# Attention pipeline: a step's scores placed ahead of its turned scores on TensorE, and the sum ahead of the exponential on ScalarE

## Chip, cores and metric

One core of a Trainium2 chip runs the whole program. The metric is the device time of one execution in microseconds (us); less is better. The times before are three executions of the kernel, and the time is their median.

## What is computed

The program is a small network over `x` of 2 x 1024 tokens with 128 features: a feed-forward part, a Mamba part, a second feed-forward part, a mixture of experts, attention, and the mixture of experts again. The change lies in the attention, which is, for each of 2 batches and 16 heads of width 64 (32 heads in all, `h` = 0 to 31):

```python
dots = einsum('bhid,bhjd->bhij', q, k) * SCALE          # 1024 x 1024 per head
diag = diagonal(softmax(dots))
keep = abs((diag - mean(diag)) / std(diag, ddof=1)) <= 1.5
valid = keep[..., :, None] & keep[..., None, :]
attn = softmax(where(valid, dots, -1e30))
attn = where(any(valid), attn, 0.0)
out = (attn @ v) @ w_out.T + b_out
```

## The kernel before

Everything stays in fp32; a product of two fp32 operands is made of three matmuls on halves rounded to fp32r (hi x hi, lo x hi, hi x lo). The engines are programmed by hand: each has its own instruction stream, executed in the order in which it is written, and semaphores tie the streams together.

**Steps.** A head is cut into 8 blocks of 128 rows or keys. All engines run over the same counter `t`, one step per block. A kind of work with offset `AT_X` handles in step `t` block `(t - AT_X) % 8` of head `(t - AT_X) // 8`. The ones that matter here:

- *Scores* (offset 0, written S(t) below): PE computes `dots` for 128 query rows into a PSUM tile of 1024 columns, in three pairs of matmuls on the two row halves of the array (L1969, L1970). DVE takes the block's diagonal out of it (`diagonal`, L2267, result `at_neg_diag`), ACT computes the exponential with that as its bias and sums each row (`sums`, L2169), which gives the diagonal of the first softmax.
- *Best* (offset 13, B(t)): one matmul pair (L2009, L2010), and DVE's masked row maximum (L2276, result `at_row_max`).
- *Turned scores* (offset 22, T(t)): PE computes the transposed block less the row maximum, four pairs (L2019, L2020 and L1890 with `at_shift_row`). ACT turns it into `at_e` (`exps`, L2179), DVE rounds that to `at_e_hi` (the cast, L2397), POOL forms the rest `at_e_lo` (L2422).
- *Weigh* (offset 24, two steps after the turned scores): PE multiplies `at_e_hi` and `at_e_lo` with the values into `at_pv_ps` (L1890), three pairs in a straight part ahead of B(t) and three in a turned part behind it.

So the streams meet in steps 22 to 255, in which a step has scores, turned scores, best and, from step 24, weigh. Before that only scores and best run, behind it only turned scores, weigh and the last of best.

**Per step, before.** PE: T(t), S(t), straight weigh, B(t), turned weigh. ACT: `exps`(t), then `sums`(t). DVE: `diagonal`(t), small statistics, the cast of `at_e`(t), best(t). Some steps have more: once per head PE projects q and k of a head (`qk`, in step 8h-3), and at the start of the next step ACT rounds it (L2154) and DVE takes the rest (L2251), ahead of that step's diagonal; in two steps of every 32 the same happens with the values of four heads (L1939; ACT L2161, DVE L2257); once in 16 steps there is an output projection, which DVE adds to `x` (L2371). Once per head ACT copies `at_pv_ps` out (L2218).

**PSUM slots.** Three tiles `at_ps0` to `at_ps2` serve all of these in turn. `attention_slots` writes down the order in which they are taken, and PE waits (`slot_free`) before a use of slot n for the reader of slot n-3: for scores the end of `sums`, for turned scores the end of `exps`, for best the end of DVE's best.

The waits that the argument needs:

```python
    # attention_act
    def sums(h, blk):
        act.wait_ge(sem["at_diag"], h * BLK + blk + 1)
    def exps(h, blk):
        act.wait_ge(sem["at_turned_scores"], e + 1)
        if e >= 2:
            act.wait_ge(sem["at_lo"], e - 2 + 1)
    # attention_dve
    def diagonal(h, blk):
        dve.wait_ge(sem["at_scores"], e + 1)
        ...
        if at := due(t, AT_TURNED, BLK):
            e = at[0] * BLK + at[1]
            dve.wait_ge(sem["at_exp"], e + 1)
```

Of the kernel before, what the change touches and what calls it, by code (L numbers as in the profile page):

```python
# [44 lines left out]
BLK = SEQ // P  # L45
# [1526 lines left out]
AT_SPLIT, AT_QK, AT_SCORES, AT_STATS, AT_MEAN, AT_SQUARE, AT_MASK, AT_BEST, AT_SHIFT = -6, -3, 0, 8, 9, 10, 11, 13, 21  # L1572
# [6 lines left out]
def due(t, offset, n=1):  # L1579

    h, k = divmod(t - offset, BLK)
    return (h, k) if 0 <= h < NH and k < n else None
# [27 lines left out]
def small_due(t):  # L1610

    for kind, offset in (("mean", AT_MEAN), ("square", AT_SQUARE), ("turn_mask", AT_MASK), ("turn_shift", AT_SHIFT)):
        if at := due(t, offset):
            return kind, at[0]
    return None


def attention_slots():

    order, number = [], {}  # L1620
    for t in range(AT_FIRST, AT_LAST):
        small, best = small_due(t), due(t, AT_BEST, BLK)
        if at := due(t, AT_TURNED, BLK):
            order.append([("turned_scores", *at)])
        if at := due(t, AT_SCORES, BLK):
            order.append([("scores", *at)])
        if small or best:
            order.append([(*small, 0)] if small else [])
            if best:
                order[-1].append(("best", *best))  # L1630
        if (h := qk_due(t)) is not None:
            order.append([("qk", h, 0)])
        if at := group_due(t):
            order.append([("values", *at)])
        if (h := pair_due(t)) is not None:
            order.append([("out", h, 0)])
    for n, keys in enumerate(order):
        for key in keys:
            number[key] = n
    return order, number  # L1640
# [230 lines left out]
def attention_pe(c, m):  # L1871
# [227 lines left out]
    for t in range(AT_FIRST, AT_LAST):  # L2099
        weighed, tested = due(t, AT_PV, BLK), due(t, AT_BEST, BLK)  # L2100
        apart = bool(weighed and tested)
        if at := due(t, AT_TURNED, BLK):
            turned_scores(*at)
        if at := due(t, AT_SCORES, BLK):
            scores(*at)
        if at := due(t, AT_MEAN):
            mean(at[0])
        if at := due(t, AT_SQUARE):
            square(at[0])
        if at := due(t, AT_MASK):  # L2110
            turn_mask(at[0])
        if at := due(t, AT_SHIFT):
            turn_shift(at[0])
        if apart:
            weigh(*weighed, False)
        if tested:
            best(*tested)
        for turned in (False, True):
            if (h := qk_due(t)) is not None:
                if apart:  # L2120
                    project(h, turned)
                elif not turned:
                    project_alone(h)
                    if h == 1:
                        fill_wait(pe, c, m.ps[2][:, HALF[0]], 27)
            if at := group_due(t):
                if apart:
                    values(*at, turned)
                elif not turned:
                    values_alone(*at)  # L2130
            if (h := pair_due(t)) is not None:
                if apart:
                    project_out(h, turned)
                elif not turned:
                    project_out_alone(h)
            if apart and not turned:
                weigh(*weighed, True)
        if weighed and not apart:
            weigh_alone(*weighed)
            if weighed == (LAST, BLK - 1):  # L2140
                fill_wait(pe, c, m.ps[(m.slot_no["out", LAST, 0] + 1) % 3][:, HALF[0]], 15)


def attention_act(c, m):
    act, sem = c.act, c.sem

    def slot(kind, h, k=0):
        return m.ps[m.slot_no[kind, h, k] % 3]

    def round_qk(h):  # L2150
        act.wait_ge(sem["at_qk"], h + 1)
        if h >= SLOTS:
            act.wait_ge(sem["at_turned_scores"], (h - SLOTS) * BLK + BLK)
        act.eng.activation(m.qk[h % SLOTS][:, HI, :], slot("qk", h)[:], ACT.Copy).then_inc(sem["at_qk_hi"])  # L2154

    def round_values(g, part):
        blks = slice(part * (BLK // 2), (part + 1) * (BLK // 2))
        act.wait_ge(sem["at_v"], 2 * g + part + 1)
        if g:
            act.wait_ge(sem["at_pv"], (g * GROUP - 1) * BLK + blks.stop)  # L2160
        act.eng.activation(m.v_hi[:, blks, :, 0, :].rearrange("p b h d -> p (b h) d"),  # L2161
                           slot("values", g, part)[:].rearrange("p (h d) -> p h d", d=HD),
                           ACT.Copy).then_inc(sem["at_v_hi"])

    def sums(h, blk):
        s = h % SLOTS
        ps = slot("scores", h, blk)
        act.wait_ge(sem["at_diag"], h * BLK + blk + 1)
        act.eng.activation(ps[:], ps[:], ACT.Exp, scale=SCALE, bias=m.small["neg_diag"][s][:, blk:blk + 1],  # L2169
                           accum_out=m.small["sums"][s][:, blk:blk + 1]).then_inc(sem["at_sum"])  # L2170

    def exps(h, blk):
        e = h * BLK + blk
        act.wait_ge(sem["at_turned_scores"], e + 1)
        act.wait_ge(sem["at_xn_lo"], NCH)
        act.wait_ge(sem["at_wv_lo"], 1)
        if e >= 2:
            act.wait_ge(sem["at_lo"], e - 2 + 1)
        act.eng.activation(m.e[e % 2][:], slot("turned_scores", h, blk)[:], ACT.Exp, scale=SCALE,  # L2179
                           bias=m.small["dropped"][h % SLOTS][:, blk:blk + 1]).then_inc(sem["at_exp"])  # L2180

    def last_inverses():

        act.wait_ge(sem["at_ones"], 2)
        for hf in range(2):
            act.eng.activation(m.last_inv[HD:, HALF[hf]], m.pv_ps[HD:, HALF[hf]], ACT.Ln,
                               bias=m.tiny[HD:, 0:1]).then_inc(sem["at_pv_out"])
            act.wait_ge(sem["at_pv_out"], LAST + 2 * hf + 1)
            act.eng.activation(m.last_inv[HD:, HALF[hf]], m.last_inv[HD:, HALF[hf]], ACT.Exp,
                               scale=-1.0).then_inc(sem["at_pv_out"])  # L2190

    def parts_of(whole, parts, done):
        act.eng.activation(parts[:, 0:1], whole[:], ACT.Copy).then_inc(sem["at_dev"])
        act.wait_ge(sem["at_dev"], done + 1)
        act.eng.activation(parts[:, 1:2], parts[:, 0:1].bitcast(F32), ACT.Identity, scale=-1.0,
                           bias=whole[:, 0:1]).then_inc(sem["at_dev"])

    def row_parts(h):
        i = h % SLOTS
        act.wait_ge(sem["at_stats"], STATS * h + 2)  # L2200
        parts_of(m.ones_col["row_sum"][i], m.halves["row_sum"][i], DEVS * h)

    def deviations(h):
        i = h % SLOTS
        act.wait_ge(sem["at_stats"], STATS * h + 3)
        act.eng.activation(m.small["dev2"][i][:], m.small["diag"][i][:], ACT.Square, bias=m.ones_col["neg_mean"][i][:, 0:1],
                           accum_out=m.ones_col["sq_sum"][i][:, 0:1]).then_inc(sem["at_dev"])
        act.wait_ge(sem["at_dev"], DEVS * h + 3)
        parts_of(m.ones_col["sq_sum"][i], m.halves["sq_sum"][i], DEVS * h + 3)

    for t in range(AT_FIRST, AT_LAST):
        if at := due(t, AT_PV_OUT):
            h = at[0]
            act.wait_ge(sem["at_pv"], h * BLK + BLK)
            if h:
                act.wait_ge(sem["at_norm"], h)
            if h < LAST:
                act.eng.activation(m.pv_sb[:], m.pv_ps[:], ACT.Copy).then_inc(sem["at_pv_out"])  # L2218
            else:
                last_inverses()  # L2220
        if (h := qk_due(t - 1)) is not None:
            round_qk(h)
            if h == 1:
                attention_later_norm_act(c, m)
        if at := group_due(t - 1):
            round_values(*at)
        if at := due(t, AT_TURNED, BLK):
            exps(*at)
        if at := due(t, AT_SCORES, BLK):
            sums(*at)  # L2230
        if at := due(t, AT_STATS):
            row_parts(at[0])
        if at := due(t, AT_MEAN):
            deviations(at[0])
    act.wait_ge(sem["x_attn"], ATTN_SUMS)
# [436 lines left out]
```

## Time and profile before

| | |
|---|---|
| three executions | 1890.33, 1894.06, 1895.96 us |
| median | 1894.06 us |
| the profiled execution: its time | 1891.39 us |
| its span, first to last instruction | 1889.9 us |
| mean granted TensorE clock | 0.990 of full |
| busy share of the span: PE, DVE, ACT, POOL | 94%, 70%, 61%, 62% |
| steps 22 to 255 of the attention | 777.0 to 1678.9 us, 234 steps |

The share of an engine is its busy time over the whole span, a mean over stages with different limits. The time of the profiled execution is 2.67 us under the median.

### The profile page before, as it was taken

The page shows a single profiled execution, that of the slowest core. Times are in us where ns is not written, and L with a number is a line of the kernel's source. Part 1 is how long each engine was busy: PE and PEld are TensorE (multiplying, and loading weights), DVE is VectorE, ACT ScalarE, POOL GpSimd, SP SyncE. Part 2 cuts the span into 40 slices and gives each one's busy share as a digit, 9 for nine tenths or more (in the row PEclk, how much of TensorE's full clock was granted, in tenths as well). Part 3 has the DMA queues.
Part 4 walks back from the last instruction along what each step waited for, and adds up shares of the span by engine and source line. Part 5 has one row for each costly group of instructions (what it writes and reads, how often), then busy time and mean ns, then how long its engine had stood idle before and what let it go on. Part 6 is the DMA issues. An engine that isn't in the chain of part 4 may idle for free. (4 is left out here: it accounts for less than half of the span.)

```text
span 1889.9 us, 29839 instructions
## 1 busy us (share of the span) xinstructions
PE 1781.0 (94%) x11031; PEld 1211.9 (64%) x11031; DVE 1330.9 (70%) x2493; ACT 1150.2 (61%) x1715; POOL 1172.7 (62%) x660
## 2 busy tenths in 40 slices
PE   9998999888999897899999999999999999999888
PEld 5883444334786674577777777777777777765466
DVE  5627899996445764777777777777777777778676
ACT  5326777853435447676767676766766676653554
POOL 5551677874554452377776776777767777677354
PEclk9999999999999999999999999999999999999999
DMA  3000000000001003121222222121212121200100
GB/s 100 1 1 1 1 0 1 1 0 1 1 1 50 1 1 100 39 60 48 60 53 55 54 54 65 44 70 42 66 36 71 48 60 47 58 24 12 50 6 17
DMA packets 43664, 66.03 MB, mean 35 GB/s; under 512 B 24768, under 2 KB 26176, under 8 KB 43264
## 3 DMA queue, kind: packets, MB, share of 16 engines
q1 hardware_dynamic: 43056, 63.54, 12.9%
q8 instruction: 88, 1.44, 0.3%
q10 hardware_dynamic: 432, 0.59, 0.1%
q14 instruction: 56, 0.46, 0.1%
q0 software_dynamic: 32, 0.00, 0.0%
HBM read 29.05 MB, written 1.24 MB: 16 GB/s over the span
## 5 line engine op out<-in xcount | busy, mean ns | idle before, releaser
L2422 POOL TENSOR_TENSOR at_e_lo<-at_e,at_e_hi 128x1024 fp32r<-128x1024 f32 x256 | 613.0, 2395 | 300.8 <-DVE at_e_hi L2397 296.4
L2179 ACT ACTIVATE at_e<-at_ps,at_dropped 128x1024 f32<-128x1024 f32 x256 | 285.6, 1116 | 222.0 <-PE at_ps L1890 201.4
L2276 DVE CUSTOM_DVE_ANT_0 at_ps<-at_ps,at_mask 128x1024 f32<-128x1024 f32 x256 | 313.3, 1224 | 4.1 <-PE at_ps L2010 4.1
L2169 ACT ACTIVATE at_ps<-at_ps,at_neg_diag 128x1024 f32<-128x1024 f32 x256 | 278.6, 1088 | 36.7 <-DVE at_neg_diag L2267 36.4
L2397 DVE CAST at_e_hi<-at_e 128x1024 fp32r<-128x1024 f32 x256 | 233.8, 913 | 23.1 <-ACT at_e L2179 19.5
L1969 PE MATMUL at_ps<-at_kq,at_qk 64*128 64x512 f32 x768 | 221.0, 395 | 8.6 <-DMA at_kq<-at_qk 3.0
L2019 PE MATMUL at_ps<-at_qk,at_kq 64*128 64x512 f32 x768 | 224.7, 399 | 1.6 <-DVE at_row_max L2276 1.2
L1890 PE MATMUL at_pv_ps<-at_e_hi,at_v_hi 64*128 64x512 f32 x980 | 225.7, 453 | 0.2 <-issue 0.2
L2020 PE MATMUL at_ps<-at_kq,at_qk 64*128 64x512 f32 x768 | 224.8, 399 | 0.0
L1970 PE MATMUL at_ps<-at_qk,at_kq 64*128 64x512 f32 x768 | 221.1, 395 | 0.0
L1056 POOL TENSOR_TENSOR mb_work<-mb_work,mb_c 128x1024 f32<-128x1024 f32 x64 | 151.8, 2373 | 97.7 <-DVE mb_work L1025 97.6
L421 POOL TENSOR_TENSOR ffn_lo<-ffn_hid,ffn_hi 128x512 fp32r<-128x512 f32 x96 | 127.2, 1328 | 132.1 <-DVE ffn_hi L338 132.1
L1890 PE MATMUL at_pv_ps<-at_e_hi,at_v_lo 64*64 64x512 f32 x980 | 195.4, 391 | 0.0
L1890 PE MATMUL at_pv_ps<-at_e_lo,at_v_hi 64*128 64x512 f32 x980 | 194.5, 389 | 0.0
L2267 DVE CUSTOM_DVE_ANT_0 at_junk_diag<-at_ps,ident 128x128 bf16<-128x128 f32 x256 | 74.0, 289 | 146.8 <-PE at_ps L1970 144.4
L1969 PEld LDWEIGHTS at_ps<-at_kq,at_qk 64*128 64x128 f32 x768 | 139.4, 185 | 47.9 <-DMA at_kq<-at_qk 12.8
L2019 PEld LDWEIGHTS at_ps<-at_qk,at_kq 64*128 64x128 f32 x768 | 139.7, 185 | 39.6 <-issue 7.9
L1500 POOL TENSOR_TENSOR moe_hid_lo<-moe_prod,moe_hid_hi 128x512 fp32r<-128x512 f32 (+1 forms) x72 | 92.8, 1290 | 95.5 <-ACT moe_hid_hi L1332 95.5
L1025 DVE TENSOR_TENSOR_SCAN mb_work<-mb_work,mb_u_ps 128x1024 f32<-128x1024 f32 x64 | 146.3, 2286 | 6.4 <-PE mb_y_ps L652 1.2
L338 DVE CAST ffn_hi<-ffn_hid 128x512 fp32r<-128x512 f32 x96 | 64.0, 670 | 120.9 <-ACT ffn_hid L309 119.6
L2020 PEld LDWEIGHTS at_ps<-at_kq,at_qk 64*128 64x128 f32 x768 | 139.7, 185 | 2.3 <-issue 1.0
L1970 PEld LDWEIGHTS at_ps<-at_qk,at_kq 64*128 64x128 f32 x768 | 139.4, 185 | 0.9
(392 smaller groups left out, 4158.7 us busy)
## 6 DMA issues: line engine op xcount, KB each, us to landing
at_kq<-at_qk SPq DMA_DIRECT2D x128, 256.0 KB, 4.0
at_mask<-at_mask_dram SPq DMA_DIRECT2D x32, 256.0 KB, 3.6
at_recips<-at_recip_row SPq DMA_DIRECT2D x31, 256.0 KB, 4.4
ffn_h_raw<-in_h SPq DMA_DIRECT2D x2, 1024.0 KB, 7.6
at_head_w_raw<-in_w_qkv SPq DMA_DIRECT2D x32, 64.0 KB, 3.9
x<-in_x SPq DMA_DIRECT2D x4, 256.0 KB, 4.7
moe_gate_in<-in_gate_in SPq DMA_DIRECT2D x2, 512.0 KB, 3.9
moe_up_in<-in_up_in SPq DMA_DIRECT2D x2, 512.0 KB, 4.4
```

Source lines behind the costliest of these rows:

```text
L1025: dve.eng.tensor_tensor_scan(m.state[i % MB_STATES_HELD], m.d_a[i % MB_DECAYS], m.u_ps[:], 0.0, ALU.mult, ALU.add).then_inc(sem["mb_scan"])
L1056: pool.eng.tensor_tensor(m.state[i % MB_STATES_HELD], m.state[i % MB_STATES_HELD], m.c_sb[i % 3], ALU.mult).then_inc(sem["mb_hc"])
L1890: mm = pe.eng.matmul(bank, w[rows], moving[rows], start=first, stop=last)
L1969: pe.eng.matmul(ps[:, HALF[0]], own[TOP, q, rows], swapped[TOP, k, HALF[0]], start=(n == 0), stop=(n == 2))
L1970: mm = pe.eng.matmul(ps[:, HALF[1]], swapped[LOW, q, rows], own[LOW, k, HALF[1]], start=(n == 0), stop=(n == 2))
L2019: pe.eng.matmul(ps[:, HALF[0]], swapped[TOP, k, keys], own[TOP, q, HALF[0]], start=(n == 0), stop=False)
L2020: pe.eng.matmul(ps[:, HALF[1]], own[LOW, k, keys], swapped[LOW, q, HALF[1]], start=(n == 0), stop=False)
L2169: act.eng.activation(ps[:], ps[:], ACT.Exp, scale=SCALE, bias=m.small["neg_diag"][s][:, blk:blk + 1], accum_out=m.small["sums"][s][:, blk: ...
L2179: act.eng.activation(m.e[e % 2][:], slot("turned_scores", h, blk)[:], ACT.Exp, scale=SCALE, bias=m.small["dropped"][h % SLOTS][:, blk:blk ...
L2276: dve.eng.tensor_tensor_reduce(out=ps[:], in0=ps[:], in1=m.mask[h % 2][:], scale=1.0, scalar=-BIG, op0=ALU.add, op1=ALU.max, accum_out=m.s ...
L2397: dve.eng.tensor_copy(m.e_hi[e % 3][:], m.e[e % 2][:]).then_inc(sem["at_hi"])
L2422: pool.eng.tensor_tensor(m.e_lo[e % 3][:], m.e[e % 2][:], m.e_hi[e % 3][:].bitcast(F32), ALU.subtract).then_inc(sem["at_lo"])
```

## The change

Three loops are written in another order; no instruction is added, removed or resized.

```diff
 # attention_slots
     for t in range(AT_FIRST, AT_LAST):
         small, best = small_due(t), due(t, AT_BEST, BLK)
+        if at := due(t, AT_SCORES, BLK):
+            order.append([("scores", *at)])
         if at := due(t, AT_TURNED, BLK):
             order.append([("turned_scores", *at)])
-        if at := due(t, AT_SCORES, BLK):
-            order.append([("scores", *at)])
 # attention_pe
+        if at := due(t, AT_SCORES, BLK):
+            scores(*at)
         if at := due(t, AT_TURNED, BLK):
             turned_scores(*at)
-        if at := due(t, AT_SCORES, BLK):
-            scores(*at)
 # attention_act
+        if at := due(t, AT_SCORES, BLK):
+            sums(*at)
         if at := due(t, AT_TURNED, BLK):
             exps(*at)
-        if at := due(t, AT_SCORES, BLK):
-            sums(*at)
```

PE at the start of a plain step in the attention, before (L2019, L2020 and L1890 are the turned scores, L1969 and L1970 the scores):

```order
3078 L2019 MATMUL at_ps<-at_qk,at_kq 128x512 [waits at_exp]
3079 L2020 MATMUL at_ps<-at_kq,at_qk 128x512
3080 L2019 MATMUL at_ps<-at_qk,at_kq 128x512
3081 L2020 MATMUL at_ps<-at_kq,at_qk 128x512
3082 L2019 MATMUL at_ps<-at_qk,at_kq 128x512
3083 L2020 MATMUL at_ps<-at_kq,at_qk 128x512
3084 L1890 MATMUL at_ps<-at_shift_row,at_minus 128x512 x2
3085 L1969 MATMUL at_ps<-at_kq,at_qk 128x512 [waits at_sum]
3086 L1970 MATMUL at_ps<-at_qk,at_kq 128x512
```

The same place in the changed kernel:

```order
3078 L1969 MATMUL at_ps<-at_kq,at_qk 128x512 [waits at_sum]
3079 L1970 MATMUL at_ps<-at_qk,at_kq 128x512
3080 L1969 MATMUL at_ps<-at_kq,at_qk 128x512
3081 L1970 MATMUL at_ps<-at_qk,at_kq 128x512
3082 L1969 MATMUL at_ps<-at_kq,at_qk 128x512
3083 L1970 MATMUL at_ps<-at_qk,at_kq 128x512
3084 L2019 MATMUL at_ps<-at_qk,at_kq 128x512 [waits at_exp]
3085 L2020 MATMUL at_ps<-at_kq,at_qk 128x512
```

The two groups have changed places, and each keeps its wait for its own PSUM reader.

ACT in the step of the statistics and the next, before (L2179 is `exps`, L2169 `sums`):

```order
528 L2179 ACTIVATE at_e<-at_ps,at_dropped 128x1024 [waits at_lo,at_turned_scores]
529 L2169 ACTIVATE at_ps,at_sums<-at_ps,at_neg_diag 128x1024 [waits at_diag]
530 L2179 ACTIVATE at_e<-at_ps,at_dropped 128x1024 [waits at_lo,at_turned_scores]
531 L2169 ACTIVATE at_ps,at_sums<-at_ps,at_neg_diag 128x1024 [waits at_diag]
532 L2179 ACTIVATE at_e<-at_ps,at_dropped 128x1024 [waits at_lo,at_turned_scores]
```

And in the changed kernel:

```order
528 L2169 ACTIVATE at_ps,at_sums<-at_ps,at_neg_diag 128x1024 [waits at_diag]
529 L2179 ACTIVATE at_e<-at_ps,at_dropped 128x1024 [waits at_lo,at_turned_scores]
530 L2169 ACTIVATE at_ps,at_sums<-at_ps,at_neg_diag 128x1024 [waits at_diag]
531 L2179 ACTIVATE at_e<-at_ps,at_dropped 128x1024 [waits at_lo,at_turned_scores]
532 L2169 ACTIVATE at_ps,at_sums<-at_ps,at_neg_diag 128x1024 [waits at_diag]
```

Within a step the sum now stands ahead of the exponential.

DVE's stream is the same in both kernels. The tail of one step and the head of the next (L2267 diagonal, L2397 cast, L2276 best, L2257 rest of the values):

```order
1006 L2397 CAST at_e_hi<-at_e 128x1024 [waits at_pv,at_exp]
1007 L2276 ISA at_ps,at_row_max<-at_ps,at_mask 128x1024 [waits at_best]
1008 L2276 ISA at_row_max 128x1
1009 L2257 TENSOR_TENSOR at_v_lo<-at_ps,at_v_hi 128x1024 [waits at_v_hi]
1010 L2267 ISA at_junk_diag,at_neg_diag<-at_ps,ident 128x128 [waits at_diag,at_scores]
1011 L2267 ISA at_neg_diag 128x1
1012 L2397 CAST at_e_hi<-at_e 128x1024 [waits at_pv,at_exp]
```

Nothing moved here: the diagonal of a step stands ahead of the step's cast, and the next diagonal behind best. POOL's and the DMA queue's streams are the same in both kernels as well.

## Rows read from the trace of the kernel before

**Rows 1.** The page: the span, and busy time, share and instructions of PE.
```profile
span 1889.9 us, 29839 instructions
PE 1781.0 (94%) x11031; PEld 1211.9 (64%) x11031; DVE 1330.9 (70%) x2493; ACT 1150.2 (61%) x1715; POOL 1172.7 (62%) x660
```

**Rows 2.** Busy time by stretch; columns as the first row says.
```profile
core 0: us, PE busy (x) PEld busy (x) DVE busy (x) ACT busy (x) POOL busy (x), PEclk, DMA share, GB/s
777.00:1678.90 901.90, 888.91 (x7558) 654.21 (x7560) 655.48 (x1575) 627.45 (x950) 645.61 (x318) 1.00 0.22 54
```

**Rows 3.** DVE in 776:1679: counts, ns min/median/max; idle before cast, before diagonal.
```profile
L2397 DVE CAST at_e_hi<-at_e x234: 650/695/2080, 777.2 to 1676.0; 128x1024 fp32r<-128x1024 f32 x117
...
  ACT at_e L2179: 8.4, 51
...
L2267 DVE CUSTOM_DVE_ANT_0 at_junk_diag<-at_ps,ident x234: 278/291/293, 777.0 to 1675.8; 128x128 bf16<-128x128 f32 x117
...
  PE at_ps L1970: 135.6, 160
```

**Rows 4.** Timeline, one plain step: start, duration (us), engine, line, idle before and releaser.
```profile
1353.41 1.12 ACT L2179 ACTIVATE at_e<-at_ps,at_dropped 128x1024 f32<-128x1024 f32 x1 [1.58 <-PE at_ps L1890]
...
1354.42 1.09 ACT L2169 ACTIVATE at_ps<-at_ps,at_neg_diag 128x1024 f32<-128x1024 f32 x1
...
1354.56 0.69 DVE L2397 CAST at_e_hi<-at_e 128x1024 fp32r<-128x1024 f32 x1 [0.17 <-ACT at_e L2179]
1355.17 1.23 DVE L2276 CUSTOM_DVE_ANT_0 at_ps<-at_ps,at_mask 128x1024 f32<-128x1024 f32 x1
1355.33 2.39 POOL L2422 TENSOR_TENSOR at_e_lo<-at_e,at_e_hi 128x1024 fp32r<-128x1024 f32 x1 [0.83 <-DVE at_e_hi L2397]
```

**Rows 5.** Timeline: a diagonal, the sum that waited for it, and ACT's next instruction.
```profile
1340.15 0.29 DVE L2267 CUSTOM_DVE_ANT_0 at_junk_diag<-at_ps,ident 128x128 bf16<-128x128 f32 x1 [1.86 <-PE at_ps L1970]
...
1340.48 1.09 ACT L2169 ACTIVATE at_ps<-at_ps,at_neg_diag 128x1024 f32<-128x1024 f32 x1 [1.03 <-DVE at_neg_diag L2267]
...
1341.50 0.19 ACT L2169 ACTIVATION_READ_ACCUMULATOR at_ps<-at_ps,at_neg_diag 128x1 f32 x1
1341.59 0.19 ACT L2193 ACTIVATE at_row_sum_parts<-at_row_sum 128x1 fp32r<-128x1 f32 x1
```

**Rows 6.** Timeline of DVE in the lead-in: best, and a diagonal that was ready behind it.
```profile
757.22 1.23 DVE L2276 CUSTOM_DVE_ANT_0 at_ps<-at_ps,at_mask 128x1024 f32<-128x1024 f32 x1 [1.83 <-PE at_ps L2010]
758.37 0.14 DVE L2276 DVE_READ_ACCUMULATOR2_ANT at_row_max<- 128x1 f32 x1
758.37 0.28 DVE L2267 CUSTOM_DVE_ANT_0 at_junk_diag<-at_ps,ident 128x128 bf16<-128x128 f32 x1
```

**Rows 7.** Timeline around a projection of q and k: PE, ACT's rounding, DVE's rest, diagonal.
```profile
1328.22 0.41 PE L1890 MATMUL at_ps<-at_xn_hi,at_head_w_hi 64*128 64x512 f32 x2
...
1328.45 0.40 PE L1890 MATMUL at_ps<-at_xn_hi,at_head_w_lo 64*128 64x512 f32 x2
...
1330.51 1.03 ACT L2154 ACTIVATE at_qk<-at_ps 128x1024 fp32r<-128x1024 f32 x1 [1.64 <-PE at_ps L1890]
...
1331.58 1.22 DVE L2251 TENSOR_TENSOR at_qk<-at_ps,at_qk 128x1024 fp32r<-128x1024 f32 x1 [1.86 <-ACT at_qk L2154]
...
1332.72 0.28 DVE L2267 CUSTOM_DVE_ANT_0 at_junk_diag<-at_ps,ident 128x128 bf16<-128x128 f32 x1
```

**Rows 8.** Timeline around the second half of the values: turned weigh, then ACT.
```profile
903.97 0.39 PE L1890 MATMUL at_pv_ps<-at_e_hi,at_v_hi 64*128 64x512 f32 x2
...
904.86 1.03 ACT L2218 ACTIVATE at_pv_sb<-at_pv_ps 128x1024 f32<-128x1024 f32 x1 [0.56 <-PE at_pv_ps L1890]
...
905.78 1.02 ACT L2161 ACTIVATE at_v_hi<-at_ps 128x1024 fp32r<-128x1024 f32 x1
```

**Rows 9.** Timeline: a cast that met POOL's work.
```profile
1299.48 2.40 POOL L2434 TENSOR_TENSOR at_heads_out<-at_pv_sb,at_recips 64x1024 f32<-64x1024 f32 x1
...
1301.28 1.15 DVE L2397 CAST at_e_hi<-at_e 128x1024 fp32r<-128x1024 f32 x1
```

**Rows 10.** Busy time by stretch in the lead-in, columns as in rows 2.
```profile
748.00:752.00 4.00, 2.34 (x14) 1.11 (x14) 1.70 (x11) 3.08 (x8) 0.00 (x0) 0.90 0.96 234
752.00:754.50 2.50, 2.50 (x14) 1.60 (x14) 0.84 (x5) 1.67 (x3) 0.00 (x0) 0.50 0.38 73
757.00:776.00 19.00, 13.03 (x84) 7.48 (x84) 14.29 (x45) 11.91 (x24) 0.00 (x0) 1.00 0.05 15
```

**Rows 11.** Timeline of PE in 752 to 754: two successive matmuls of one array half.
```profile
752.61 0.62 PE L1969 MATMUL at_ps<-at_kq,at_qk 64*128 64x512 f32 x1
...
753.03 0.62 PE L1969 MATMUL at_ps<-at_kq,at_qk 64*128 64x512 f32 x1
```

## The prediction

> **What bounds the kernel now.** I read the page first, then the stretch of the attention by busy time, then the order of the four streams, and last the timeline of single steps. The page has PE busy for 94% of the span [rows 1]. In the stretch where all kinds of attention work run together, steps 22 to 255, PE is busy 888.9 of 901.9 us, while DVE is busy 655.5, ACT 627.5 and POOL 645.6 [rows 2]. So PE sets the pace there, and a step costs 901.9 / 234 = 3.85 us on average (234 by the counts of [rows 3]). The reader should see two things in that. First, at most 901.9 - 888.9 = 13.0 us can be won here by feeding PE better. Second, the three other engines have slack, but slack of an engine is not slack of a chain that runs through several engines: what matters is how long the longest ring of waits is that has to be gone round once per step.
>
> **The rings, before.** DVE does in a step: diagonal(t), cast(t), best(t). ACT does exp(t), sum(t). The cast needs exp(t), the sum needs diagonal(t). In the plain step of [rows 4] the exponential starts at 1353.41, the cast at 1354.56, best at 1355.17, and the sum follows the exponential without holding any of them up. The diagonal of the next step waits behind best, but the exponential of that step does not wait for that diagonal; it waits for PE ("1.58 <-PE"). A ring through diagonal, sum, exp, cast, best and the next diagonal exists, but it spans two steps: the sum of step t stands ahead of the exponential of step t+1. DVE has time to spare in it: it sat idle 135.6 us before the diagonal, in 160 cases, for PE [rows 3].
>
> **The change on ACT.** Here is the whole of the matter. With the sum ahead of the exponential of its own step, and DVE's order as it was, the ring closes within one step: diagonal(t) on DVE, sum(t) on ACT, exp(t) on ACT, cast(t) on DVE, best(t) on DVE, diagonal(t+1). Each element is queued behind the one before it or waits for it, and no buffer can loosen that, because DVE reaches diagonal(t+1) only behind best(t). Its length, start to start:
>
> - diagonal to the sum waiting for it: 1340.15 to 1340.48, 0.33 us [rows 5].
> - sum to ACT's next instruction, past the accumulator read: 1340.48 to 1341.59, 1.11 us [rows 5].
> - exponential to the cast that waits for it: 1353.41 to 1354.56, 1.15 us [rows 4].
> - cast to best: 0.61 us [rows 4].
> - best to a diagonal that is ready: 757.22 to 758.37, 1.15 us [rows 6].
>
> The sum is 4.35 us per step. That is more than the average step of 3.85 with all its additions, and much more than a plain one. So the ring becomes the bound, and PE waits.
>
> **What PE does meanwhile.** I checked that PE doesn't lengthen the ring. Counting from diagonal(t): successive pairs start 0.23 us apart [rows 7]. B(t) starts at about 0.15, when the previous best is out; the turned weigh follows to 1.2; S(t+1) needs sum(t), whose accumulator read ends at 1.54, and runs 1.6 to 2.3; T(t+1) needs exp(t), started at 1.44 and 1.12 long, and runs 2.6 to 3.5; the straight weigh to 4.2; then B(t+1) waits for best(t). S(t+1) is wanted at 4.35 and T(t+1) at 5.79. Both have two microseconds in hand. So the earlier scores, the PE half of the change, cost nothing and give nothing: their diagonal has to wait for DVE anyway. The small statistics stand between diagonal and cast, where DVE now idles about two microseconds, and cost nothing. The transfers of q, k and shift rows have longer steps to land in, so their waits go.
>
> **What still adds to the ring.** DVE work that stands ahead of a diagonal isn't covered.
>
> - q and k: the projection takes its slot three behind, which is now the scores' (it was the turned scores'), so it starts at sum(t)'s end, 1.6. From its first matmul to ACT's rounding are 2.29 us, to DVE's rest 1.07 more, to the diagonal 1.14 more [rows 7]: 1.6 + 4.50 = 6.10 instead of 4.35, so 1.75 us. 28 of these in the stretch (h = 4 to 31): 49.0 us.
> - values, first half: the same shape, 1.75, 8 times: 14.0 us.
> - values, second half: ACT has the copy of `at_pv_ps` ahead of the rounding. Turned weigh at 2.3, copy 0.89 later, rounding 0.92 later [rows 8], then 1.07 and 1.14 as above: 6.32, so 1.97, 8 times: 15.8 us.
> - output projection: PE's part is done by the time best ends, DVE's addition of about 1.15 us (the 1.14 of rows of the same size) stays, 13 times: 15.0 us.
>
> **The sum.** 234 x 4.35 + 49.0 + 14.0 + 15.8 + 15.0 = 1017.9 + 93.8 = 1111.7 us for the stretch, against 901.9: 209.8 us longer. The steps ahead of it and behind it have no turned scores or no scores, so their streams are the same, and nothing is counted there. The profiled execution would go from 1891.4 to 2101 us; the median lies 2.7 above that execution, so the forecast is 1894.1 + 209.8 = 2104 us. The error to be expected: a step 0.1 shorter gives 2081; all additions at their bare DVE time of 1.14 give 57 x 1.14 = 65.0, so 29 us less, 2075; at twice their size, 94 more, 2198, which I find far because each link of them was read.
>
> **Two prices that rows bound from both sides.** The cast is 0.65 to 2.08 us long, median 0.70 [rows 3]. It is long when it meets POOL: at 1301.28 it took 1.15, with POOL's `at_heads_out` still running to 1301.88 [rows 9]. In the ring, POOL's `at_e_lo` starts 0.77 behind the cast's start and lasts 2.39 [rows 4], so it ends 3.16 behind it, 1.19 ahead of the next cast. I take the free value, 0.61 to best; the other end is 0.46 more in each step, 108 us. The Trainium skill, in "SBUF — State Buffer", section "Who interferes with whom", says that of two such instructions the later is blocked for all of the earlier; the rows agree with it, and by it the sum stays as it is unless POOL runs late by that 1.19 us.
>
> The second is TensorE's clock. In the stretch it was 1.00 throughout at 98.6% busy [rows 2]. Afterwards PE would be busy 889 of 1112 us, 80%, with three short pauses a step. The nearest rows speak for a clock that stays: 757 to 776 had 13.0 of 19.0 us busy at 1.00, but 752 to 754.5 had 0.50 (1.2 GHz), right behind a stretch busy only 2.34 of 4.0 us [rows 10]. I take 1.00. The Trainium skill, in "TensorE: Matmul & The Clock Gate", section "A second HAM failure mode: psum-queue depth-cycling", says that a kernel which pauses between groups while it cycles PSUM banks swings between the two levels. That speaks against this kernel; the rival below prices it.
>
> **The rivals.**
>
> - *The ring does not close, and PE gets its scores' readers earlier.* This would be so if the round trip were shorter than 3.85 us, for instance if DVE's diagonal could pass a waiting cast. Then what remains of the change is that the diagonal comes four pairs, 0.9 us, earlier, and some of the 135.6 us of DVE's waiting and PE's 13.0 us go: 1881 to 1894 us. Against it: even without any of the semaphore time, by durations alone, the ring is 0.29 + 1.09 + 1.12 + 0.69 + 1.23 = 4.42, and less the overlaps of neighbours on one engine about 4.0, over 3.85. 3%.
> - *The casts meet POOL* in every step: 2104 + 108 = 2212 us. For it: the 2.08 maximum; against it: the 1.19 us of room. 6%; in part of the steps it lies between.
> - *The clock falls to 1.2 GHz in the attention.* Then pairs start 0.42 us apart [rows 11], 14 pairs a step are 5.9 us, PE is the bound again, and if that held throughout the stretch would be 234 x 1.5 = 360 us longer still, 2465; in a third of the steps, 2225. Against it: the 19 us at 69% busy and full clock. 5%.
> - *The additions hide* in the ring more than I see, or the links are each some hundredths shorter: 2060 to 2080. 6%.
>
> **How the numbers follow.** The forecast's own case has 80%: 2104 us, with about 2080 to 2150 around it. The range is drawn to 2078 and 2165, so that it takes in links a tenth shorter and casts that meet POOL in half of the steps, and leaves out most of the rivals. A difference of 0.3%, 5.7 us, is about what a measurement of this kernel can tell. Faster by more than that 0.02 and within it 0.01, both from the first rival; slower 0.97.
>
> **What would show it.** In the profile of the changed kernel: ACT's sum waits for the diagonal in nearly all of 234 steps; the cast waits for the exponential about 2 us each (it was 8.4 us in all the stretch, in 51 cases [rows 3]); DVE's idle before the diagonal for PE is almost gone; PE is busy about 80% of the stretch and waits for `at_sum`, `at_exp` and `at_row_max`; diagonals are 4.35 us apart in plain steps, and about 1.7 more behind a projection. The stretch is about 1112 us, and the stages outside it unchanged within a microsecond or two. The prediction is wrong if the diagonals are 3.3 us apart in plain steps (no ring), if casts last over 1 us, or if the clock shows less than 1.00 there.

## The result and the profile after

| | before | changed |
|---|---|---|
| median | 1892.68 us (4 executions) | 2103.32 us (4 executions, 2102.09 to 2104.64) |
| ratio, with its 95% interval | | 1.1117 [1.1104, 1.1131] |
| span of the profiled execution | 1889.9 us | 2100.8 us |
| steps 22 to 255 | 902 us | 1114 us |
| mean granted TensorE clock | 0.990 | 0.991 |

The forecast was 2104 us in a range of 2078 to 2165, a growth of 209.8 us; measured are 210.6. Of all executions that the runs below rest on two were slow, one of the kernel before (2846.07 us) and one of it with a small instruction more (2438.51 us, granted clock 0.65), and no ratio rests on them.

First the page of the changed kernel, which answers to [rows 1]:

```profile
span 2100.8 us, 29839 instructions
PE 1875.1 (89%) x11031; PEld 1205.4 (57%) x11031; DVE 1289.2 (61%) x2493; ACT 1145.5 (55%) x1715; POOL 1170.3 (56%) x660
```

The stretch of the joint steps, which answers to [rows 2], with the same columns (us, then busy time and count of PE, PEld, DVE, ACT, POOL, then the granted clock):

```profile
774.80:1888.60 1113.80, 983.74 (x7562) 647.61 (x7562) 614.31 (x1575) 624.11 (x950) 642.65 (x318) 1.00 0.18 44
```

It is 211.9 us longer than before (1113.8 against 901.9), and the span is 210.9 longer, so everything outside the stretch is unchanged within about a microsecond. No engine got more instructions. One plain step in the timeline of the changed kernel, DVE and ACT, to be laid beside [rows 4 to 6]:

```profile
1505.65 0.28 DVE L2267 CUSTOM_DVE_ANT_0 at_junk_diag<-at_ps,ident 128x128 bf16<-128x128 f32 x1
...
1505.97 1.09 ACT L2169 ACTIVATE at_ps<-at_ps,at_neg_diag 128x1024 f32<-128x1024 f32 x1 [1.20 <-DVE at_neg_diag L2267]
...
1507.08 1.11 ACT L2179 ACTIVATE at_e<-at_ps,at_dropped 128x1024 f32<-128x1024 f32 x1
...
1508.22 0.69 DVE L2397 CAST at_e_hi<-at_e 128x1024 fp32r<-128x1024 f32 x1 [1.97 <-ACT at_e L2179]
1508.83 1.23 DVE L2276 CUSTOM_DVE_ANT_0 at_ps<-at_ps,at_mask 128x1024 f32<-128x1024 f32 x1
...
1509.97 0.29 DVE L2267 CUSTOM_DVE_ANT_0 at_junk_diag<-at_ps,ident 128x128 bf16<-128x128 f32 x1
```

These starts are 0.32, 1.11, 1.14, 0.61 and 1.14 us apart, 4.32 together. Who waits for whom in the stretch shows the same ring (engine, waiting, waited for: us in total, times, longest):

```profile
DVE at_e_hi L2397 <- ACT at_e L2179: 432.8, 233, 2.3
ACT at_ps L2169 <- DVE at_neg_diag L2267: 428.2, 234, 3.4
...
PEld at_ps L1969 <- ACT at_ps L2169: 43.0, 66, 0.7
ACT at_qk L2154 <- PE at_ps L1890: 42.6, 28, 1.5
PEld at_ps L2019 <- ACT at_e L2179: 42.2, 101, 0.5
```

The cast now waits for ACT in 233 of 234 steps (51 before, [rows 3]), ACT's sum waits for DVE in all 234, and DVE no longer waits for PE before a diagonal at all. DVE and ACT each wait some 430 us for the other. That is what a closed ring looks like: two engines at 55% of their time, each idle because of the other.

### The profile page after: what moved, and what is told of

It reads as the page before. It is cut to its first block and busy times, and to the rows that moved or that the text cites. A ratio compares the mean times of both kernels' runs of the same rounds, so it can differ in the third digit from the quotient of the medians.

```text
span 2100.8 us, 29839 instructions
## 1 busy us (share of the span) xinstructions
PE 1875.1 (89%) x11031; PEld 1205.4 (57%) x11031; DVE 1289.2 (61%) x2493; ACT 1145.5 (55%) x1715; POOL 1170.3 (56%) x660
## 3 DMA queue, kind: packets, MB, share of 16 engines
HBM read 29.05 MB, written 1.24 MB: 14 GB/s over the span
## 5 line engine op out<-in xcount | busy, mean ns | idle before, releaser
L2169 ACT ACTIVATE at_ps<-at_ps,at_neg_diag 128x1024 f32<-128x1024 f32 x256 | 278.6, 1088 | 437.2 <-DVE at_neg_diag L2267 436.9
L2397 DVE CAST at_e_hi<-at_e 128x1024 fp32r<-128x1024 f32 x256 | 201.8, 788 | 446.4 <-ACT at_e L2179 443.9
L2276 DVE CUSTOM_DVE_ANT_0 at_ps<-at_ps,at_mask 128x1024 f32<-128x1024 f32 x256 | 313.7, 1226 | 4.3 <-PE at_ps L2010 4.2
L2179 ACT ACTIVATE at_e<-at_ps,at_dropped 128x1024 f32<-128x1024 f32 x256 | 283.6, 1108 | 41.9 <-PE at_ps L1890 25.4
L1969 PE MATMUL at_ps<-at_kq,at_qk 64*128 64x512 f32 x768 | 235.8, 414 | 26.7 <-ACT at_ps L2169 19.9
L2019 PE MATMUL at_ps<-at_qk,at_kq 64*128 64x512 f32 x768 | 234.4, 411 | 5.1 <-DVE at_row_max L2276 1.8
L1970 PE MATMUL at_ps<-at_qk,at_kq 64*128 64x512 f32 x768 | 236.3, 415 | 0.0
L2020 PE MATMUL at_ps<-at_kq,at_qk 64*128 64x512 f32 x768 | 233.8, 410 | 0.0
L1890 PE MATMUL at_pv_ps<-at_e_hi,at_v_hi 64*128 64x512 f32 x980 | 223.5, 443 | 0.8 <-DVE at_e_hi L2397 0.8
L1890 PE MATMUL at_pv_ps<-at_e_lo,at_v_hi 64*128 64x512 f32 x980 | 199.0, 390 | 0.0
L1890 PE MATMUL at_pv_ps<-at_e_hi,at_v_lo 64*64 64x512 f32 x980 | 198.9, 390 | 0.0
L1969 PEld LDWEIGHTS at_ps<-at_kq,at_qk 64*128 64x128 f32 x768 | 134.3, 186 | 91.4 <-ACT at_ps L2169 47.8
L2019 PEld LDWEIGHTS at_ps<-at_qk,at_kq 64*128 64x128 f32 x768 | 130.0, 185 | 78.1 <-ACT at_e L2179 43.3
L652 PE MATMUL mb_y_ps<-mb_work,ident 128*128 128x512 f32 x256 | 131.8, 601 | 8.3 <-DVE mb_dtx L949 6.8
L1970 PEld LDWEIGHTS at_ps<-at_qk,at_kq 64*128 64x128 f32 x768 | 134.3, 187 | 2.7
L2020 PEld LDWEIGHTS at_ps<-at_kq,at_qk 64*128 64x128 f32 x768 | 130.0, 185 | 2.7
```

The lines of the kernel that those rows point to most:

```text
L1890: mm = pe.eng.matmul(bank, w[rows], moving[rows], start=first, stop=last)
L1969: pe.eng.matmul(ps[:, HALF[0]], own[TOP, q, rows], swapped[TOP, k, HALF[0]], start=(n == 0), stop=(n == 2))
L1970: mm = pe.eng.matmul(ps[:, HALF[1]], swapped[LOW, q, rows], own[LOW, k, HALF[1]], start=(n == 0), stop=(n == 2))
L2019: pe.eng.matmul(ps[:, HALF[0]], swapped[TOP, k, keys], own[TOP, q, HALF[0]], start=(n == 0), stop=False)
L2020: pe.eng.matmul(ps[:, HALF[1]], own[LOW, k, keys], swapped[LOW, q, HALF[1]], start=(n == 0), stop=False)
L2276: dve.eng.tensor_tensor_reduce(out=ps[:], in0=ps[:], in1=m.mask[h % 2][:], scale=1.0, scalar=-BIG, op0=ALU.add, op1=ALU.max, accum_out=m.s ...
```

## The experiments

All distances between diagonals below are read from DVE's diagonals (L2267) in the timeline of each kernel, steps 22 to 255, as means over the steps with the same `t mod 8` (us). Step 3 has the output projection every second time, 5 the projection of q and k; 6 and 7 are those without values, and without step 254, which has more to do (5.56 in the changed kernel).

| t mod 8 | 0 | 1 | 2 | 4 | 5 | 6 | 7 |
|---|---|---|---|---|---|---|---|
| before | 3.22 | 3.42 | 3.42 | 3.31 | 5.34 | 2.99 | 3.71 |
| changed | 4.32 | 4.33 | 4.33 | 4.32 | 6.20 | 4.32 | 4.33 |
| PE half alone | 3.77 | 4.19 | 4.20 | 3.99 | 7.73 | 2.66 | 4.28 |
| ACT half alone | 4.53 | 4.53 | 4.53 | 4.53 | 7.18 | 4.52 | 4.53 |
| changed, best ahead of the cast | 3.48 | 3.41 | 4.76 | 3.26 | 6.17 | 3.18 | 3.42 |

**The two halves apart.** The first kernel has only the order of PE and of the slots:

```diff
-        if at := due(t, AT_TURNED, BLK):
-            turned_scores(*at)
         if at := due(t, AT_SCORES, BLK):
             scores(*at)
+        if at := due(t, AT_TURNED, BLK):
+            turned_scores(*at)
```

> Only the PE half: scores ahead of turned scores in the slots and on PE; ACT keeps the exponential ahead of the sum. Theory R, as predicted (the slowdown is the ring diagonal, sum, exp, cast, best, closed on ACT alone; the PE half costs nothing): no ring in one step, so 1881 to 1894 us. Rival P (PE's order closes a ring of its own over the PSUM slot): T(t)'s last pair starts 1.5 us behind S(t)'s first, exp starts 0.43 later, the sum 1.01 behind it and ends 1.28 later, and only then S(t+1) may write the slot: 4.2 to 4.3 us per plain step, relaxed in the steps after an extra slot, so 2040 to 2110 us, with PE waiting for at_sum (L2169) before L1969.

Measured: 2096.98 us, 1.1095 [1.1075, 1.1114] of before. The rival is right, and by its numbers: a plain step is 4.19 us. From its timeline:

```profile
1505.19 1.11 ACT L2179 ACTIVATE at_e<-at_ps,at_dropped 128x1024 f32<-128x1024 f32 x1 [1.16 <-PE at_ps L1890]
...
1506.20 1.08 ACT L2169 ACTIVATE at_ps<-at_ps,at_neg_diag 128x1024 f32<-128x1024 f32 x1
...
1507.19 0.20 ACT L2169 ACTIVATION_READ_ACCUMULATOR at_ps<-at_ps,at_neg_diag 128x1 f32 x1
...
1507.45 0.50 PE L1969 MATMUL at_ps<-at_kq,at_qk 64*128 64x512 f32 x1 [0.59 <-ACT at_ps L2169]
```

The exponential waits for the turned scores, the sum (whose diagonal has long been there) stands behind it, and the next step's scores wait for the sum to give back the PSUM tile; the turned scores stand behind those scores. The starts of exponential, sum and scores are 1.01 and 1.25 us apart, and the next exponential starts 1.93 us after the scores, at 1509.38: 4.19 together. It is a second ring, through PE, ACT and a slot, without DVE. The steps with a projection of q and k grew most, from 5.34 to 7.73, which is 70 of the 206 us.

The second has only ACT's order:

```diff
-        if at := due(t, AT_TURNED, BLK):
-            exps(*at)
         if at := due(t, AT_SCORES, BLK):
             sums(*at)
+        if at := due(t, AT_TURNED, BLK):
+            exps(*at)
```

> Only the ACT half: the sum ahead of the exponential; slots and PE as before. Theory R: the ring is there whatever PE does, 4.32 us a plain step, 2100 us. A finer reading of R: here T(t+1), which waits for exp(t), stands ahead of S(t+1) on PE, so the diagonal comes exp(t)'s end plus seven pairs (1.5 us) plus 0.43 us later: about 4.5 us a step, and the projections start at the exponential's end instead of the sum's, 1 us later 44 times: 2150 to 2195 us, with DVE idle before the diagonal for PE (L1970). If the ACT half were harmless: 1893 us.

Measured: 2210.47 us, 1.1691 [1.1671, 1.1710], above the finer reading's end by 15 us. The step is 4.53, as it said. From its timeline:

```profile
1501.26 1.11 ACT L2179 ACTIVATE at_e<-at_ps,at_dropped 128x1024 f32<-128x1024 f32 x1
...
1502.42 0.49 PE L2019 MATMUL at_ps<-at_qk,at_kq 64*128 64x512 f32 x1 [0.40 <-ACT at_e L2179]
...
1503.91 0.39 PE L1969 MATMUL at_ps<-at_kq,at_qk 64*128 64x512 f32 x1
...
1504.35 0.29 DVE L2267 CUSTOM_DVE_ANT_0 at_junk_diag<-at_ps,ident 128x128 bf16<-128x128 f32 x1
```

The turned scores start when the exponential has left their tile, the scores follow, and the diagonal comes 0.44 us after the last pair, 0.2 later than best (read accumulator 1504.15) would have allowed it. One point was off: DVE's wait was expected to be listed under PE; it is too short in most steps and stands there with 15 us only, over the whole execution. The excess over the range is where the expectation added nothing: a step with an output projection takes 7.03 us, 2.50 more than a plain one, against 1.22 more in the changed kernel, which over 13 of them is 17 us. Each half alone costs 206 and 320 us; together they cost 211. So the halves are not additive: with the sum first, the early scores are worth 107 us.

**The ring opened on DVE.** The changed kernel, with two blocks of DVE's loop exchanged, and the kernel before with the same exchange:

```diff
+        if at := due(t, AT_BEST, BLK):
+            best(*at)
         if at := due(t, AT_TURNED, BLK):
             ...
             dve.eng.tensor_copy(m.e_hi[e % 3][:], m.e[e % 2][:]).then_inc(sem["at_hi"])
-        if at := due(t, AT_BEST, BLK):
-            best(*at)
```

> The changed kernel, and on DVE best(t) ahead of the cast of its step, all else equal. The same instructions on every engine. Theory R: best (1.15 us) leaves the ring and runs while DVE waits for the exponential; the ring is 0.33 + 1.11 + 1.15 + about 0.6 = 3.2 us, under PE's own 3.3 in a plain step, so PE is the bound again: 1880 to 1915 us. If the loss came from the order on PE, from the clock or from contention, it stays near 2100.

> The kernel before, with only DVE's best(t) ahead of the cast. Shows what that order is worth by itself: PE is the bound there with 13 us of idle in the stretch, so 1885 to 1905 us; a gain in e3 over this one would be the scores' order, a loss its cost.

Measured: 1974.01 us, 1.0437 [1.0420, 1.0455], and 1905.08 us, 1.0075 [1.0058, 1.0091]. One instruction moved out of the ring takes 129 us off the changed kernel, and plain steps fall from 4.32 to between 3.18 and 3.5, as expected. But the time is 59 us above the end of the forecast's range, for two reasons that the distances show: step 2 lasts 4.76 (39 us more than before over the stretch), and steps 5 and those with values keep the lengths of the changed kernel (6.17, and 6.13 and 6.41 with values, against 5.34, 4.94 and 5.12 before; the means with values include steps 22 and 23), since their projections still wait in PE's slot order for the sum (steps 5 to 7 are 42 us more than before). Moving best is no gain in itself: it costs the kernel before 14 us (1890.76 without the exchange), with 4.12 for 3.42 in step 2 and 4.19 for 4.55 in step 3. Against that kernel the changed order still costs 69 us, 3.6%.

**A small instruction more.** The same DVE instruction in three places; it reads the identity and writes a column that nothing reads:

```diff
         if at := due(t, AT_BEST, BLK):
             best(*at)
+        if due(t, AT_SCORES, BLK) and due(t, AT_TURNED, BLK):
+            dve.eng.tensor_reduce(m.pad[t % 8][:], c.ident[:], AX.X, ALU.add)
```

> The changed kernel with one small extra instruction on DVE (a row sum over 128 columns of the identity into an unused column, about 0.2 us by the spacing of the diagonal) behind best in each of the 234 joint steps, ahead of the next diagonal. Theory R: it is on the ring, and every step grows by its length: 234 x 0.2 = 47 us, 2140 to 2160 us. If DVE were not on the path (PE or PSUM slots set the pace): no change, 2103.

> The same extra instruction in the changed kernel, but right behind the diagonal, ahead of the cast, where DVE waits over 2 us for the exponential. Theory R: hidden, 2103 us within 6. If DVE's total work counted: as p1.

(there the two new lines stand behind `diagonal(*at)`)

> The kernel before with the extra instruction behind best, as in p1. Theory R: there the ring spans two steps and PE is the bound; DVE sat idle 136 us before its diagonals in 160 steps, so most of it is absorbed: 1892 to 1905 us.

> Only the PE half (as the first experiment), with the small DVE instruction behind best in each joint step. If that kernel's bound is the ring turned scores, exp, sum, slot, scores, which has no DVE in it: within 8 us of 2097. If it were DVE's ring through best, as in the full change: 33 us more, 2130.

| kernel | without | with |
|---|---|---|
| changed, behind best | 2103.3 | 2136.85, 1.1288 [1.1269, 1.1307] of before |
| changed, behind the diagonal | 2103.3 | 2102.02, 1.1103 [1.1084, 1.1121] |
| before, behind best | 1892.1 | 1893.69, 1.0000 [0.9989, 1.0011] |
| PE half alone, behind best | 2097.0 | 2098.30, 1.1088 [1.1071, 1.1105] |

Where it stands in the timeline of the first:

```profile
1502.24 0.28 DVE L2401 TENSOR_REDUCE at_pad<-ident 128x1 f32<-128x128 f32 x1
1502.44 0.28 DVE L2267 CUSTOM_DVE_ANT_0 at_junk_diag<-at_ps,ident 128x128 bf16<-128x128 f32 x1
```

It takes 0.20 us of DVE's time, and the plain step grows from 4.32 to 4.52. The total grew by 33.5 and not by 47, 3 us below the expected range, because in step 5 and in those with values DVE waits behind it anyway (6.20 with and without). The other three places cost nothing that can be told from zero. These four are the sharpest evidence of the study: the same instruction is paid in full ahead of the diagonal and free right behind it, 0.3 us later; and it is free behind best where only PE's order was changed, so that kernel, as slow as the full change, is slow by a ring that this place on DVE is not in.

**What held step 2.** In the third kernel's trace the `keeps` instruction L2306 (128x8) stands out:

```profile
L2306 DVE TENSOR_SCALAR at_keep<-at_dev,at_limit,at_varies x32: 291/1382/2074, 751.6 to 1766.1; 128x8 f32<-128x8 f32 x32
```

(ns: shortest, median, longest; before it is 290, 299, 920.) Two kernels put it elsewhere in DVE's step. Behind the cast:

```diff
             negate_square(at[0])
-            keeps(at[0])
 ...
             dve.eng.tensor_copy(m.e_hi[e % 3][:], m.e[e % 2][:]).then_inc(sem["at_hi"])
+        if at := due(t, AT_SQUARE):
+            keeps(at[0])
```

> The changed kernel with best ahead of the cast, and the four small instructions of keeps (once per head) behind the cast. In the version without that, its third one took 1.38 us instead of 0.3 beside POOL's at_e_lo, and steps of t mod 8 = 2 lasted 4.76 us instead of 3.4. If POOL's work over the shared port is the cause and the cast starts POOL anew behind it: 1.0 to 1.3 us less in 29 heads, 1936 to 1945 us. If those instructions only waited for something on PE or ACT: 1974.

and, together with the two reciprocal instructions, between best and the cast:

```diff
         if at := due(t, AT_BEST, BLK):
             best(*at)
+        if at := due(t, AT_SQUARE):
+            keeps(at[0])
+        if (at := due(t, AT_RECIP)) and at[0] < LAST:
+            ...
```

> The changed kernel with DVE's order diagonal, best, then keeps and the two small reciprocal instructions, then the cast (third experiment, with the statistics moved behind best but ahead of the cast). POOL's at_e_lo of the step before is then nearly over when keeps starts, 3.0 us behind the previous cast's start against its end at 3.16. If the shared port is what held keeps (1.38 us in the third experiment, 2.21 in the one with it behind the cast): keeps takes 0.3 to 0.5 us, steps of t mod 8 = 2 last 4.1 to 4.5 instead of 4.76, the clock stays at 1.00, and the time is 1955 to 1970 us. If something on PE or ACT held it, keeps stays long and the time at 1974 or above.

The first came out the other way from its forecast: 2089.78 us, 1.1050 [1.1033, 1.1067], 116 us slower than the kernel it was to mend. The second: 1964.34 us, 1.0379 [1.0362, 1.0397], 10 us faster, in its range. From the timeline of the first of them:

```profile
1504.10 0.69 DVE L2398 CAST at_e_hi<-at_e 128x1024 fp32r<-128x1024 f32 x1
1504.86 2.34 POOL L2423 TENSOR_TENSOR at_e_lo<-at_e,at_e_hi 128x1024 fp32r<-128x1024 f32 x1 [1.31 <-DVE at_e_hi L2398]
1505.02 2.21 DVE L2306 TENSOR_SCALAR at_keep<-at_dev,at_limit,at_varies 128x8 f32<-128x8 f32 x1
1507.26 0.17 DVE L2309 TENSOR_SCALAR at_dropped<-at_keep 128x8 f32<-128x8 f32 x1
...
1507.49 0.26 PE L1984 MATMUL at_ps<-ident,at_dropped 64*8 64x64 f32 x2 [3.25 <-DVE at_dropped L2309]
1507.59 0.79 PE L1890 MATMUL at_pv_ps<-at_e_hi,at_v_hi 64*128 64x512 f32 x2
```

An instruction on eight columns takes 2.21 us, and ends when POOL's does (1507.23 and 1507.20). In the third kernel it was the same: there `keeps` started at 1499.31, took 1.38 us and ended at 1500.69, and POOL's `at_e_lo` at 1500.66. The expectation had said that the cast "starts POOL anew behind it", and drew the wrong conclusion: right behind the cast is the one place where `keeps` is sure to meet all of `at_e_lo`. With it between best and cast, the median is 291 ns again, and step 2 is 4.42 us. That `keeps` is blocked for what is left of POOL's instruction is what the Trainium skill says in "SBUF — State Buffer", section "Who interferes with whom"; here 2.21, 1.38 and 0.29 us in three places agree with it. In the kernel with `keeps` behind the cast PE waits 3.25 us for the result (28 of 29 times; once 2.39), and its clock falls behind most of these waits.

The table's distances, taken for this kernel too, split its 116 us. Step 2 went from 4.76 to 7.12, 68 us over the stretch. Steps 3 and 4 grew by 36 and 7 us. In the 5 of 29 heads where the clock stayed at 1.00 behind the wait, step 2 is as long or nearly as long (7.15; 6.28 in the first), but steps 3 and 4 are as in the third kernel (3.19 to 3.22 and 3.32 or 3.33); in the other heads without an output projection step 3 takes 4.15 to 4.89. So about 68 us are the wait and about 43 the lower clock.

**Is the opposite direction better?** Since the change moved the scores earlier and lost, the last two moved them later in the kernel before, behind the straight weigh:

```diff
-        if at := due(t, AT_SCORES, BLK):
+        late = apart and t % BLK in (4, 6, 7) and due(t, AT_SCORES, BLK)
+        if (at := due(t, AT_SCORES, BLK)) and not late:
             scores(*at)
 ...
         if apart:
             weigh(*weighed, False)
+        if late:
+            scores(*late)
```

> The kernel before, with the scores moved the other way: behind the straight weigh, ahead of best, in the steps of t mod 8 = 4, 6, 7, which have no small product. Then four pairs instead of one lie between straight and turned weigh, and the pause before the turned weigh (0.1 us between pairs) goes in those; the sum and diagonal start 0.7 us later, for which the order exp, sum has room (diagonal to sum's end 1.6 us, needed 3.3 later). Gain about 60 x 0.1 = 6 us, with the pauses for the transfer of q and k untouched: 1883 to 1889 us beside 1892. If the later diagonal lengthens a ring: over 1892.

> The same also in the steps of t mod 8 = 0, where the first scores of a head wait for the transfer of q and k (0.86 us in the row read). The straight weigh would cover that wait, but it waits itself for ACT's copy of at_pv_ps there. Gain over the former 0 to 15 us: 1870 to 1887 us.

Measured: 1891.08 us, 1.0000 [0.9991, 1.0009], no change; and 1913.44 us, 1.0118 [1.0102, 1.0133], slower. In the first, PE's waits for its own straight weigh did shrink as meant, from 34.7 us in 146 cases to

```profile
PEld at_pv_ps L1890 <- PE at_pv_ps L1890: 21.5, 95, 0.3
...
PEld at_ps L1969 <- DMA at_kq<-at_qk: 14.1, 21, 1.4
...
PEld at_ps L1969 <- ACT at_ps L2172: 6.4, 29, 0.2
```

but 6.4 us of waits for the sum of a delayed step are new, and the wait for the transfer of q and k grew from 11.7 to 14.1 us in the weight loads and by 1.7 in the matmuls. The gain was given back within the head. In the second the straight weigh waits for ACT's copy of `at_pv_ps`, as feared: in one such step the copy ends at 1350.85 and the weigh starts at 1350.95, after 0.76 us without a matmul. The profile names no releaser for these waits (16 us in 21 cases); the kernel's order and this distance do. No version that ran beats the kernel before.

## Why the prediction was right, and where not

- *The ring.* Right in kind and size: 4.35 us predicted, 4.32 measured; 234 x 0.03 = 7 us too much.
- *The additions.* Projection of q and k: 1.75 predicted, 6.27 - 4.32 = 1.95 in a typical case. Its first matmul starts 1.68 us behind the diagonal, not 1.6, and the path to ACT is 2.39, not 2.29. Values: 1.75 and 1.97 predicted, 1.90 and 2.10 measured. Output: 1.15 predicted, 1.22 measured (5.54 in 11 of its 13 steps, 5.60 in two). Over 57 cases these are about 9 us too little. The two errors cancel nearly, and the stretch came out at 1113.8 for 1111.7. The good agreement of the total is partly luck.
- *PE's share.* Predicted 80% of the stretch, measured 983.7 of 1113.8, 88%. The step that failed is "PE would be busy 889": the busy time isn't a constant of the work. The first matmul after a pause is listed with 0.49 us instead of 0.39, and matmuls that overlapped each other's ends before now stand apart.
- *"So the earlier scores, the PE half of the change, cost nothing and give nothing."* This is the sentence that the runs refute. Alone, they cost 206 us by a ring that the prediction never looked for, and beside the sum's new place they give 107. What is true is less: in the changed kernel S(t+1) and T(t+1) are ready before the ring needs them. The total was right since, with the sum first, PE's ring is not closed: S(t+1) waits for a sum that stands ahead of the exponential. The third kernel shows it, as it has the same order on PE and ACT and plain steps of 3.18 to 3.5 us, where PE's ring alone had made them 4.19.
- *The rival of a gain* needed a diagonal that passes a waiting cast, or a shorter round trip. Neither is in the trace: the cast waited for the exponential in 233 of 234 steps, with the next diagonal behind it, and the round trip was 4.32. But the third kernel shows that closing wasn't the only danger: with that ring opened, the order still loses 4.4%.
- *Contention.* Casts stayed at 0.69 us (median 694 ns, one of 1923), so that rival had no part. *The clock* stayed at 1.00 in the stretch.

## What to carry to other kernels

When two instructions of one step change places on an in-order engine, ask for every instruction queued behind them on any engine which step's result it needs. A ring that spanned two steps may span one, and its length is then the price of each step, however idle the engines are. Write down the rings of an order, PSUM slots included, with their start-to-start distances; the trace of the kernel before has each of them, and the sum forecast a plain step here to 0.03 us. Halves of such a change must be judged apart and together, as they can compensate each other.

An instruction of 0.2 us put in at a suspected place tells cheaply whether that place is on the ring.

## What was not expected of the hardware

- A DVE instruction on 128x8 elements took 2.21 us when it started 0.16 us behind POOL's `at_e_lo`, and 0.29 when POOL was idle. The size of the victim says nothing about what it can lose.
- In the kernel with `keeps` behind the cast the mean granted clock over the joint steps was 0.94. PE stood still for 3.25 us in one piece once per head, and behind 24 of the 29 such pauses the clock fell to the 1.2 GHz level, some 120 us in all; matmuls are listed there with 0.62 to 0.79 us, as at that level in [rows 10, 11]. Behind the other 5 it stayed at 1.00, and what tells the two kinds apart was not found.
- The length of a pause alone doesn't decide it. With ACT's half alone (0.99) the clock fell behind 6 of 16 pauses of 1.94 to 2.05 us. With PE's half alone it stayed up behind some 40 pauses of 1.35 us in the joint steps, but fell once at their start, at 784 us, behind one of 1.24. In the changed kernel it was 1.00 throughout, with no pause over 1.27 us and about 1.1 us of waiting in a plain step (4.32 less 14 pairs at 0.23).
- The rival on the clock feared the sum of many short pauses, for which the Trainium skill, "TensorE: Matmul & The Clock Gate", section "A second HAM failure mode: psum-queue depth-cycling", gives a case. In the changed kernel such pauses did not bring the clock down.
